# Order of the first packing, of the layers' start, and of q, k and the last product with v in a layer's tile

## What is computed

```
heads:   q,k,v = x@Wq.T+bq, x@Wk.T+bk, x@Wv.T+bv     16 heads of 16
         attn  = softmax(q k^T / 4, axis = heads)     (over the heads, not over the keys)
         x_a   = layernorm(x + (attn @ v) @ Wo.T + bo)
layers (twice):
         h = second half of the channels taken from the token before (shift)
         q,k,v = split(h @ wqkv)                      8 heads of 64
         q = rotate(q/|q| * q_scale), k alike         rotary with a scale by position
         o = local attention, windows of 128: each query sees its window and the one before
         x = x + o @ wo
         h = layernorm(shift(x)) * g + b
         a, g = split(h @ w1 + b1);  x = x + (a * gelu(g)) @ w2 + b2
out:     layernorm(x + x_a)
```

## Time and profile before

| | us |
|---|---|
| median of 3 runs | 4155.8 (4153.17 to 4156.33) |
| the profiled execution | 4154.04 |
| its span, first to last instruction | 4152.3 |
| TensorE busy (PE) | 3909.4, 94% |
| VectorE busy (DVE) | 3028.8, 73% |
| ScalarE busy (ACT) | 2889.8, 70% |
| GpSimd busy (POOL) | 2171.2, 52% |
| mean granted TensorE clock | 0.989 of full speed |

### The profile page before, as it was taken

One profiled execution on the slowest core, in us unless ns is written; L12 is line 12 of the kernel. 1 busy time (PEld: TensorE's weight loads), 2 busy tenths in 40 slices (PEclk: granted clock), 3 DMA queues, 4 the chain that ended last, 5 costly groups with the idle time before them and its releaser, 6 DMA issues.

```text
span 4152.3 us, 95963 instructions
## 1 busy us (share of the span) xinstructions
PE 3909.4 (94%) x36004; PEld 3299.3 (79%) x36064; DVE 3028.8 (73%) x7348; ACT 2889.8 (70%) x7337; POOL 2171.2 (52%) x2168
## 2 busy tenths in 40 slices
PE   5999999999999689999999999999999999999997
PEld 3777777777777568888888888888888888888886
DVE  3888888888888666666666666666777777777775
ACT  3667777677766467777777777777777777777765
POOL 3999999999999623333333333323333333333332
PEclk8999999999999899999999999999999999999999
DMA  5453445445443100000000000000000000000000
GB/s 109 72 75 65 70 69 79 61 69 75 71 70 55 52 27 17 15 17 20 17 15 17 20 17 17 19 28 17 22 21 28 20 25 20 30 20 25 20 25 25
DMA packets 175106, 159.26 MB, mean 38 GB/s; under 512 B 22194, under 2 KB 173620, under 8 KB 174644
## 3 DMA queue, kind: packets, MB, share of 16 engines
q1 hardware_dynamic: 174644, 153.13, 19.6%
HBM read 52.40 MB, written 25.17 MB: 19 GB/s over the span
## 4 chain that ended last, share of the span: by engine, by line
PE 40%; ACT 11%; issue 8%; DVE 3%; POOL 3%; SPq 0%; DMA 0%; POOLq 0%; DVEq 0%; ACTq 0%
PE b_X L1452 11%; PE b_F L1521 5%; PE b_M L1574 5%; PE b_S L1472 4%; PE b_F L1600 4%; PE b_S L1482 3%; PE b_M L1493 3%; ACT L1180 2%; PE b_M L1565 2%; ACT L1186 2%; ACT b_hn L1095 1%; ACT b_g L1180 1%; ACT b_PT L1218 1%; DVE b_qT L1253 1%; DVE b_kT L1253 1%
## 5 line engine op out<-in xcount | busy, mean ns | idle before, releaser
L361 ACT ACTIVATE a_p<-a_S 128x512 f32<-128x512 f32 x1024 | 528.8, 603 | 225.4 <-PE a_S L547 225.4
L261 POOL TENSOR_TENSOR a_z<-a_p 128x1024 f32<-128x1024 f32 x256 | 604.6, 2362 | 106.7 <-ACT a_p L361 102.4
L1452 PE MATMUL b_X<-b_wqkv,b_hT 128*128 128x512 f32 x2304 | 648.4, 417 | 1.3 <-DVE b_hT L1288 1.3
L1521 PE MATMUL b_F<-b_hnT,b_w 128*128 128x256 f32 (+1 forms) x4224 | 584.9, 287 | 5.8 <-issue 5.8
L1212 ACT ACTIVATE b_p<-b_S,b_nb 128x256 f32<-128x256 f32 (+1 forms) x1024 | 444.6, 446 | 178.6 <-DVE b_nb L1264 178.5
L1521 PEld LDWEIGHTS b_F<-b_hnT,b_w 128*128 128x128 f32 (+1 forms) x4224 | 532.9, 187 | 18.5 <-issue 6.2
L1452 PEld LDWEIGHTS b_X<-b_wqkv,b_hT 128*128 128x128 f32 x2304 | 416.6, 190 | 99.8 <-issue 21.8
L989 POOL TENSOR_TENSOR b_t<-b_t 128x512 f32<-128x512 f32 x128 | 165.6, 1294 | 554.8 <-DVE b_t L1236 554.8
L425 DVE TENSOR_TENSOR a_p<-a_p,a_O 128x1536 f32<-128x1536 f32 x256 | 446.7, 1745 | 4.5 <-ACT a_O L335 4.0
L410 DVE TENSOR_REDUCE a_low_max<-a_S 128x128 f32<-128x1024 f32 x256 | 313.1, 1223 | 166.0 <-PE a_S L537 166.0
L1264 DVE CUSTOM_DVE_ANT_0 b_S<-b_S,b_mask,b_rn 128x256 f32<-128x256 f32 (+1 forms) x1024 | 399.8, 450 | 1.2 <-PE b_S L1472 1.2
(11 more groups left out here) (154 smaller groups left out, 8888.0 us busy)
## 6 DMA issues: line engine op xcount, KB each, us to landing
a_q<-a_parts SPq DMA_DIRECT2D x256, 128.0 KB, 5.0
a_k<-a_parts SPq DMA_DIRECT2D x256, 128.0 KB, 5.0
a_x<-in_x SPq DMA_DIRECT2D x16, 512.0 KB, 4.0
a_xr<-in_x SPq DMA_DIRECT2D x64, 128.0 KB, 4.7
x_after_heads<-a_n SPq DMA_DIRECT2D x64, 128.0 KB, 2.7
b_x<-x_after_heads SPq DMA_DIRECT2D x16, 512.0 KB, 4.1
x_after_layer<-b_xo SPq DMA_DIRECT2D x32, 256.0 KB, 2.3
b_x<-x_after_layer SPq DMA_DIRECT2D x16, 512.0 KB, 4.1
```

What stands on the lines that cost most here:

```text
L261: nc.gpsimd.tensor_tensor(z8[:], e[:, 0:8], e[:, 8:16], ALU.add).then_inc(s_zt, 1)
L361: nc.scalar.activation(probs[u % NE][:, hs], S[:, hs], ACT.Exp, scale=HDIM ** -0.5).then_inc(s_exp, 1)
L1452: last = nc.tensor.matmul(X[i][:], hT_of(k, a), wqkv[:, b, k, i * INNER:(i + 1) * INNER], start=(k == 0 and (a, b) == PART_PAIRS[0]), stop ...
L1521: last = nc.tensor.matmul(F[i % 2][0:size, part], w1[:, a, k, col:col + size], hnT[:, b, k, hf * 2 * P:(hf + 1) * 2 * P], start=(k == 0 an ...
```

## The change

Three parts. Heads: the packs of the first sequence are made for the first 256 columns of q and k ahead of the last 256, in DMAs of both `ot` at once where both are ready; eight of them (k, `ot` 1) are issued from ScalarE; the first layer's weights are loaded behind them. TensorE waits for the first columns before unit 0, for k's rest before unit 2 and for q's rest before unit 8. Start of the layers: SP loads x first, then tables and scales (semaphore of their own), then the second layer's weights; wqkv is split in thirds; GpSimd fills zero_col and hT1 first and a_sb and hs last, and engines wait for 3 fills where they waited for 14; VectorE makes the second layer's table behind the first products of the rotation. Layers: TensorE's `times_v(T - 1, w1_, 1)` stands ahead of `transpose_h`, and ScalarE's copies of q and k ahead of `layernorm`.

```diff
@@ -182,6 +184,17 @@
+    FIRST, REST = slice(0, SEQ // 2), slice(SEQ // 2, SEQ)
+    PACKED_REST = 16 * len(TERMS)
+    PACKED_FIRST = (PACKED_REST, 2 * PACKED_REST)
+
+    def first_pack(engine, which, ots, cols, signal):
+
+        for t, (of_k, of_q) in enumerate(TERMS):
+            part = of_k if which else of_q
+            engine.dma_start(qk8[0][which][16 * t:16 * t + 16, :, ots, cols], parts[which][:, part, ots, cols]
+                             ).then_inc(signal[which], 16)
+
     def written_out(n, u, after):
@@ -221,13 +234,18 @@
             sp.dma_start(b_rows[t:t + 1], b_terms[0:1, t]).then_inc(s_bor, 16)
+        sp.wait_ge(s_pt, CT)
+        load_x(1)
+        sp.wait_ge(s_part, part_count(0, 1, 2))
+        first_pack(sp, 0, slice(0, CT), FIRST, s_first)
+        sp.wait_ge(s_part, part_count(0, 2, 2))
+        first_pack(sp, 1, slice(0, 1), FIRST, s_first)
+        sp.wait_ge(s_part, part_count(0, 3, 2))
+        first_pack(sp, 1, slice(0, CT), REST, s_rest)
+        first_pack(sp, 0, slice(0, CT), REST, s_rest)
         if W0 is not None:
...
             load_raw(sp, raw, w, 0, s_w0)
-        sp.wait_ge(s_pt, CT)
-        load_x(1)
-        for i in range(4):
-            pack(0, 0, i)
@@ -314,6 +332,8 @@
                 act.wait_ge(s_pt, 8 * n + 3 + i)
+                if n == 1:
+                    act.wait_ge(s_rest[which], PACKED_REST)
             else:
@@ -339,6 +359,8 @@
             part_of_qk(0, i, part)
+        act.wait_ge(s_part, part_count(0, 3, 2))
+        first_pack(act, 1, slice(1, CT), FIRST, s_first)
         act.wait_ge(s_pz, 3)
@@ -528,8 +550,12 @@
             if u == 0 and b == 0:
-                for of in s_pack[par]:
-                    pe.wait_ge(of, PACKED * (r + 1))
+                for of in s_pack[par] if n else []:
+                    pe.wait_ge(of, PACKED * (r + par))
+                for which in range(2) if n == 0 else []:
+                    pe.wait_ge(s_first[which], PACKED_FIRST[which])
+            if n == 0 and b == 0 and u in (TILES // 2, UNITS // 2):
+                pe.wait_ge(s_rest[1 if u == TILES // 2 else 0], PACKED_REST)
             qt, kt = u // TILES, u % TILES
@@ -854,7 +882,8 @@
-    WEIGHTS = 16 * (LAYER_LOADS + 1 + 8)
+    WEIGHTS, SCALES = 16 * LAYER_LOADS, 16 * (1 + 8)
+    READY, MASKS, FILLED = 3, 11, 14
@@ -917,17 +946,16 @@
-        start_layer_loads(sp, W[1], w, 1, s_w)
-        sp.dma_start(base_tab[:], w["tab"].rearrange("(t p) k d -> p t k d", p=P)).then_inc(s_w, 16)
-        H = LDIM // 2
+        load_x(0, 0, 0, 0)
+        sp.dma_start(base_tab[:], w["tab"].rearrange("(t p) k d -> p t k d", p=P)).then_inc(s_scales, 16)
         for layer in range(LAYERS):
...
                 row = w[name][layer]
-                sp.dma_start(srow[layer][:, 2 * i], row.partition_broadcast(P)).then_inc(s_w, 16)
+                sp.dma_start(srow[layer][:, 2 * i], row.partition_broadcast(P)).then_inc(s_scales, 16)
                 swapped = w[name + "_swapped"][layer]
-                sp.dma_start(srow[layer][:, 2 * i + 1], swapped.partition_broadcast(P)).then_inc(s_w, 16)
-        load_x(0, 0, 0, 0)
+                sp.dma_start(srow[layer][:, 2 * i + 1], swapped.partition_broadcast(P)).then_inc(s_scales, 16)
+        start_layer_loads(sp, W[1], w, 1, s_w)
@@ -1008,20 +1036,22 @@
...
-        pool.wait_ge(s_c, 10)
+        pool.wait_ge(s_c, 7)
@@ -1133,28 +1163,31 @@
-        split_high(0)
-        act.wait_ge(s_w, WEIGHTS)
-        act.wait_ge(s_c, 14)
+        src, high, _ = split_weights(0)
+        for i, signal in enumerate((s_first_high, s_first_high, s_high)):
+            cols = slice(i * INNER, (i + 1) * INNER)
+            nc.scalar.activation(high[:, :, cols], src[:, :, cols], ACT.Copy).then_inc(signal, 1)
+        act.wait_ge(s_c, READY)
         evacuate_hT(-1, 3)
...
         evacuate_v(0, 0)
+        act.wait_ge(s_w, WEIGHTS)
...
                 live, feed = tile_exists(T), seq_exists(n - 1)
-                if tile_exists(T - 2):
-                    layernorm(T - 2, p, (w_ - 2) % TILES, par if w_ >= 2 else 1 - par)
                 if live:
...
                                          ).then_inc(s_qkTe, 1)
+                if tile_exists(T - 2):
+                    layernorm(T - 2, p, (w_ - 2) % TILES, par if w_ >= 2 else 1 - par)
                 if feed:
@@ -1288,17 +1321,30 @@
-        dve.wait_ge(s_c, 14)
-        split_low(0)
-        low_hT(-1, 3)
-        dve.wait_ge(s_w, WEIGHTS)
-        for layer in range(LAYERS):
+        def tables(layer):
+
             need(dve, s_tab, TILES * layer)
...
                 nc.vector.tensor_tensor(tab[layer][:, t], base_tab[:, t], srow[layer], ALU.mult).then_inc(s_tab, 1)
+
+        src, high, low = split_weights(0)
+        for i, (ready, signal) in enumerate(((s_first_high, s_first_split), (s_first_high, s_first_split),
+                                             (s_high, s_split))):
+            if i == 2:
+                dve.wait_ge(s_c, READY)
+                low_hT(-1, 3)
+            cols = slice(i * INNER, (i + 1) * INNER)
+            dve.wait_ge(ready, min(i + 1, 2) if i < 2 else 1)
+            nc.vector.tensor_tensor(low[:, :, cols], src[:, :, cols], high[:, :, cols], ALU.subtract).then_inc(signal, 1)
+        dve.wait_ge(s_scales, SCALES)
+        tables(0)
+        dve.wait_ge(s_tab, TILES)
+        rot_products(0, 0, 0)
+        tables(1)
         dve.wait_ge(s_tab, LAYERS * TILES)
-        rot_products(0, 0, 0)
         scale_k(0, 0)
+        dve.wait_ge(s_w, WEIGHTS)
+        dve.wait_ge(s_c, FILLED)
@@ -1441,7 +1487,7 @@
             pe.wait_ge(s_hTl, t + 1)
-            if isinstance(t, int) and t % (TILES * SEQS) == 0:
+            if isinstance(t, int) and t > 0 and t % (TILES * SEQS) == 0:
                 pe.wait_ge(s_split, SPLITS.index(("wqkv", layer)) + 1)
@@ -1524,14 +1570,17 @@
-        pe.wait_ge(s_w, WEIGHTS)
-        pe.wait_ge(s_c, 14)
+        pe.wait_ge(s_c, READY)
         tile_parity["next"] = 0
...
         projection_ready(0, 0)
+        pe.wait_ge(s_first_split, 1)
         project(0, s_q)
+        pe.wait_ge(s_first_split, 2)
         project(1, s_k)
+        pe.wait_ge(s_split, 1)
         project(2, s_v)
+        pe.wait_ge(s_w, WEIGHTS)
@@ -1551,11 +1600,11 @@
                     hidden(T, 0, w_, layer)
-                if tile_exists(T + 1) or tile_exists(T - 2):
-                    transpose_h(T, n, w_, par)
                 if tile_exists(T - 1):
...
                     times_v(T - 1, w1_, 1)
+                if tile_exists(T + 1) or tile_exists(T - 2):
+                    transpose_h(T, n, w_, par)
                 if live:
```

More of the change, by code:

```diff
@@ L113, in head_attention @@
     s_pack = [[sem(f"packed_{n}{i}") for n in "qk"] for i in range(2)]
+    s_first = [sem(f"first_packed_{n}") for n in "qk"]
+    s_rest = [sem(f"rest_packed_{n}") for n in "qk"]
     s_S = sem("scores")
@@ L764, in layers @@
     t2 = [sb(f"t2{i}", [P, LHEADS, LDIM]) for i in range(2)]
-    srow = [t2[0][:, 4 * i:4 * i + 4] for i in range(LAYERS)]
     ss = sb("ss", [P, 2 * LHEADS])
@@ L779, in layers @@
     oU = sb("oU", [P, IH, P])
+    srow = [oU[:, 2 * i:2 * i + 2].rearrange("p a (b d) -> p (a b) d", d=LDIM) for i in range(LAYERS)]
     oT = sb("oT", [P, IH, P])
@@ L802, in layers @@
     s_tab = sem("tables")
+    s_scales = sem("tables_and_scales_loaded")
+    s_first_high, s_first_split = sem("first_weights_high"), sem("first_weights_split")
     s_x = [sem(f"x_loaded{i}") for i in range(2)]
@@ L1010, in _ @@
         nc.gpsimd.memset(zero_col[:], 0.0).then_inc(s_c, 1)
+        for i in range(2):
+            nc.gpsimd.memset(hT1[i][:].bitcast(F32), 0.0).then_inc(s_c, 1)
         nc.gpsimd.memset(three_halves[:], 1.5).then_inc(s_c, 1)
@@ L1013, in _ @@
         for i in range(2):
-            nc.gpsimd.memset(hT1[i][:].bitcast(F32), 0.0).then_inc(s_c, 1)
-            nc.gpsimd.memset(a_sb[i][:], 1.0).then_inc(s_c, 1)
             nc.gpsimd.memset(mask[i][:], 0.0).then_inc(s_c, 1)
-        nc.gpsimd.memset(hs[:], 0.0).then_inc(s_c, 1)
-        pool.wait_ge(s_c, 10)
+        pool.wait_ge(s_c, 7)
         for i in range(2):
@@ L1024, in _ @@
                                     base=0, pattern=[[1, P]], channel_multiplier=-1).then_inc(s_c, 1)
+        for i in range(2):
+            nc.gpsimd.memset(a_sb[i][:], 1.0).then_inc(s_c, 1)
+        nc.gpsimd.memset(hs[:], 0.0).then_inc(s_c, 1)
         rotate(0)
```

## The result

The kernel after takes 4106.41 us (median of 4 runs, 4105.9 to 4107.66), the kernel before 4155.61 (4 runs): ratio 0.9879, 95% interval 0.9867 to 0.9891. Forecast were 4092 us in a range of 4072 to 4132: faster, as said, by 49 us instead of 63, inside the range and 2 us past the forecast's own part of it (4080 to 4104). The profiled execution took 4106.15 us; its span went from 4152.3 to 4104.4, by 47.9.

What follows compares the result with a forecast made beforehand. TensorE was taken to bound the layers, with rest left in waits and two starts. Layers 43.5 + heads' packing 12.8 + layers' start 7.2 = 63.5 us, from 4155.8 to 4092.3; range 4072 to 4132, own part 4080 to 4104.

Steps and rivals of the forecast that it cites:

- What bounds it: TensorE bounds the layers, busy 97.6% in the first and 95.7% in the second; reordering can give its idle time.
- Odd tile, `w_` 1: Layers: GpSimd's spread ends last; R (transposes of the inverses) starts 1.02 us earlier in the first layer, 1.04 in the second.
- Odd tile, `w_` 3, first layer: R (transposes of the inverses) starts 0.70 us earlier; ScalarE's in-order chain of hT copies, then oU, arrives last.
- Even tiles: Layers, `w_` 0 and 2: later hT copies and oU make R (transposes of the inverses) 0.32 and 0.22 us late.
- First packing: Heads' start: 2.1 MB at 141 GB/s; first scores at 43 us instead of 55.77, 12.8 gained.
- Layers' start: With x loaded first, TensorE's first transposes in the layers start 7.2 us earlier, between 4 and 9.
- The sum: Whole kernel: layers 43.5, heads' packing 12.8 and layers' start 7.2 make 63.5 us gained.
- 1: Layers' even tiles pay in full, later hT copies delaying everything behind by 0.87: layers gain 5 us, 4131; chance 12%.
- 2: Layers slower: ScalarE's in-order queue holds hT, oU and hnT 0.87 us later at 128 tiles; 4186 us; chance 6%.
- 3: Heads' packs cost by rows, not bytes: 8 us lost instead of 12.8 won; 4113 us; chance 8%.
- The cover that they doubted: Even tiles: ScalarE's 0.54 us wait before the exps absorbs hn's copies ending 0.5 later; hT's low part still arrives in time.
- Rival 4: Layers' even tiles lose nothing: 17 us more gained, 4075 us; chance 10%.

Runs made afterwards that it cites:

- oU first: Kernel after with ScalarE's copy oU moved ahead of its two hT copies in the layers: 4078.69 us, ratio 0.9817.
- the swap of oU: ScalarE's copy oU moved ahead of its hT copies: 4078.69 us with both moves, 4166.45 with v alone, 4181.62 with q and k alone, 4178.59 on starts alone.

## Why the prediction was right, and where its size was off

- *What bounds it*: right. TensorE's rest in the layers and the two starts are where the time came from. But a sequence gained 0.77 us in the first layer, less than the 1.0 to 1.8 of the forecast, and 1.27 in the second.
- *Odd tile, `w_` 1*: 1.02 forecast, 1.03 measured; GpSimd's spread ends last there, as worked out. Second layer 1.04 forecast, 1.09 and 1.07 measured.
- *Odd tile, `w_` 3, first layer*: 0.70 forecast, 0.59 measured, by the chain hT, oU that was named.
- *Even tiles*: the term that failed. 0.32 and 0.22 were forecast, 0.48 and 0.37 to 0.42 measured. The chain was the right one: oU first takes the loss away and leaves the rest, but for `w_` 3 of the first layer, where the same chain ends last and 0.3 more comes free. Its length was short in each link. Against the forecast in tile `w_` 0, counted from F's end (0.09 ahead of times_v): hn's transposes end at 1.77 instead of 1.71 (those of x take 0.27, not 0.21), oU at 2.81 instead of 2.73, and R starts at 2.95 instead of 2.78. The last is the largest: I took the hand-over from oU to R as 0.05, and it is 0.14 (oU done at 1994.81, R's weight load at 1994.92, its products at 1994.95). The 64 even tiles, short by 0.15 to 0.20 each, make 10.7 us, 16 odd ones of `w_` 3 1.8 more, and the other odd ones give 1.4 back: to rounding the 10.9 us by which the steady layers (32.6) fell short of 43.5.
- *First packing*: 12.8 forecast, 7.5 at the scores and 7.8 at the stage's end. That fewer bytes come sooner stands, as halving them gave 8.9 and cutting q's again 2.3. The rate was the error: with the second halves held, the first 2.1 MB land 18.9 us behind the point at which I started them (1.5 behind the first issue), which is 111 GB/s where I had 141 and 14.9 us: 4.0 us of the miss. The second halves took 3.4 us, within the up to 4.2 that I had named but 1.3 more than the 2.1 that choosing 43 had left for them. Together 5.3, the distance from 43 to 48.29. Why the rate is lower stays open: whole rows of 1 KB moved at 126 and 141 in two kernels, so the row's size alone does not say it.
- *Layers' start*: 7.2 forecast; 7.8 at the first transposes (x landed in 3.8 us, not 4.1 to 4.6), 6.5 at the third projection. Part of what is lost between is the granted clock: twelve products of a projection take 5.03 us there for 4.39 before.
- *The sum*: 10.9 + 5.0 + 0.7 short and 1.0 over at the layers' ends are the 15.6 us from 63.5 to 47.9. Nearly all errors point the same way, so it was not luck that kept the time in its range.
- *Rivals*: 1, 2 and 3 did not come. The cover that they doubted holds in the kernel after, but it is thin: with times_v behind hn's transposes a late hT costs 0.45 in every tile. Rival 4 has the right sign for a kernel with one more edit: there it is 4078.7, against its 4075.

What the sum hid is that the moves are not terms. On top of the starts alone, v ahead costs 38.7 us, q and k ahead gain 20.0, and both gain 37.7; the swap of oU gains 27.7 with both and 16.4 with v alone, and costs 34.5 alone and 57.5 with q and k alone. The slow sequences of layer 2 are in these numbers: by the distances without them v ahead costs 27 us, and the swap gains 22 with v alone and costs 27 alone.

## What to carry to other kernels

When the order of a step is changed on one engine, work out for each other in-order engine what its next instruction waits for, and put its independent copies in the order in which their sources now arrive: here that was worth more than half as much again as the change (27.7 us behind 49). Try moves together, as each alone may be a loss. Cut the bytes that the first consumer waits for before cutting what shares the queue with them.

## What the runs showed of the hardware

What a wait costs is nearer to what the weight load shows than to what the matmul does. Where R waits for oU, the matmul's row has 0.36 and the weight load's 0.47, and the tile is 0.48 longer. The swap with q and k alone adds waits for hT of 0.21 (matmul) and 0.45 (weight load) a tile, and the tiles are 0.46 to 0.5 longer than without it. In the kernel with only q and k ahead the list has 16.0 us for TensorE and 27.6 for its weight loads (0.33 and 0.56 a tile), and the even tiles are 0.4 to 0.5 longer.

```profile
PEld b_X L1480 <- ACT b_hn L1125: 27.6, 49, 0.6
```

The granted clock can fall to 0.50 inside a layer behind a wait (1.46 us where it was looked at), which costs 1.4 to 1.6 us each time; in the kernel after, with waits up to 0.4, no sequence shows it. Its four executions lie within 1.8 us of each other, with a mean granted clock of 0.989 to 0.990; thirteen of the kernel before, with waits up to 1.0, lie between 4149.4 and 4166.4 us, and that of 4166.4 has the lowest mean clock, 0.985; its profiled execution has no such sequence. A kernel that takes such waits away can gain more than their sum, and one that lengthens them (v alone ahead) can lose more.

Packs into 16 partitions moved at 141 GB/s in the kernel before and 126 behind the new order, both in rows of 1 KB; in rows of 512 bytes the first halves moved at 110 by themselves and at 130 with the second halves among them. What sets the rate between 110 and 141 no run separates.
